# Token-table products ahead of the last early shared step, and their weighted one-hots written by ScalarE, in a two-layer attention and mixture-of-experts kernel

## The reference, cut to what matters

```python
logits = xf @ router_w.T + router_b
top_vals, top_idx = jax.lax.top_k(logits, K)          # K = 4 of E = 32
rw = jax.nn.softmax(top_vals, axis=-1) * SCALE
combine = jnp.einsum('tke,tk->te', jax.nn.one_hot(top_idx, E), rw)
g = silu(einsum('th,eih->tei', xf, gate_w)); u = einsum('th,eih->tei', xf, up_w)
routed = jnp.einsum('tei,ehi,te->th', g * u, down_w, combine)
shared = silu(xf @ shared_gate_w.T) * (xf @ shared_up_w.T) @ shared_down_w.T
return routed + shared
```

## Time and profile before

| | us |
|---|---|
| median of 3 runs | 398.67 (398.26, 398.67, 399.49) |
| the profiled execution | 398.21 |
| its span, from first to last instruction | 396.4 |
| busy: PE, DVE, ACT, POOL | 330.4, 271.0, 194.0, 180.7 |
| mean granted TensorE clock | 0.952 of full speed |

### The profile page before, as it was taken

How to read it: one execution, slowest core, us unless ns; L and a number is a source line. 1 busy time by engine, 2 the same in 40 slices (tenths; PEclk the granted TensorE clock), 3 DMA queues, 4 the chain that set the end, 5 groups by cost and what they waited for, 6 DMA issues and landing times.

```text
span 396.4 us, 8440 instructions
## 1 busy us (share of the span) xinstructions
PE 330.4 (83%) x2392; PEld 193.7 (49%) x2392; DVE 271.0 (68%) x842; ACT 194.0 (49%) x452; POOL 180.7 (46%) x321
## 2 busy tenths in 40 slices
PE   0007877777999999999999959999877689998997
PEld 0006763443455555555555756666553345554455
DVE  2998869724676766666667596999877246677374
ACT  1349544335455555555551047999921255552110
POOL 2000002266677777777744145666600547774200
PEclk9999957989999999999999979999995899999999
DMA  8999999616933333333563679910011213331441
GB/s 240 345 253 340 251 336 247 166 55 180 310 106 98 105 99 108 107 102 97 131 219 134 239 262 276 223 44 2 2 50 58 79 53 95 109 94 63 155 154 53
DMA packets 35038, 59.88 MB, mean 151 GB/s; under 512 B 4178, under 2 KB 23346, under 8 KB 34994
## 3 DMA queue, kind: packets, MB, share of 16 engines
q1 hardware_dynamic: 26850, 40.41, 34.9%
q0 software_dynamic: 6528, 17.83, 14.8%
q10 hardware_dynamic: 1616, 1.11, 1.0%
HBM read 47.28 MB, written 12.06 MB: 150 GB/s over the span
## 4 chain that ended last, share of the span: by engine, by line
PE 63%; DVE 15%; issue 6%; DMA 5%; POOL 5%; ACT 5%; DVEq 1%; ACTq 0%; SPq 0%; POOLq 0%
PE bank L1388 21%; PE bank L1417 7%; PE bank L1249 6%; PE bank L1431 4%; PE bank L1400 4%; PE bank L1370 4%; PE bank L1482 3%; PE bank L1470 3%; DMA xg<-m_xn,tab 2%; POOL xg L515 2%; PE bank L1262 2%; DMA x_sb<-x 2%; DVE x_sb L1068 1%; PE bank L1162 1%; PE bank L1288 1%
## 5 line engine op out<-in xcount | busy, mean ns | idle before, releaser
L1388 PE MATMUL bank<-arena,xT 128*64 x272 | 94.4, 491 | 2.2 <-ACT xT L647 2.2
L1390 PE MATMUL bank<-xn,xT 128*64 128x384 f32 (+1 forms) x272 | 94.5, 492 | 0.0
L515 POOL DMA_INDIRECT xg<-m_xn,tab x68 | 66.2, 973 | 52.4 <-DVE tab L909 24.8
L504 POOL DMA_INDIRECT m_ys<-ysb,dest x68 | 67.8, 997 | 34.7 <-issue 18.0
L636 ACT ACTIVATE xn<-arena 128x768 f32 (+1 forms) x68 | 56.2, 827 | 18.3 <-issue 17.8
L1388 PEld LDWEIGHTS bank<-arena,xT 128*64 128x64 f32 x272 | 35.0, 139 | 43.9 <-issue 43.9
L992 DVE COPY ysb<-bank 128x256 f32<-128x256 f32 x68 | 26.1, 420 | 39.3 <-PE bank L1433 39.1
L654 ACT ACTIVATE sg<-bank 128x192 f32<-128x192 f32 (+1 forms) x71 | 22.7, 319 | 37.6 <-PE bank L1390 31.7
L647 ACT ACTIVATE xT<-bank 128x512 f32<-128x512 f32 (+1 forms) x36 | 21.3, 592 | 36.0 <-PE bank L1370 36.0
L959 DVE COPY xn<-arena 64x256 f32 (+1 forms) x136 | 36.6, 307 | 1.0
L1417 PE MATMUL bank<-arena,hT 128*64 x136 | 35.0, 380 | 1.7 <-DVE dn L955 1.7
(11 more groups left out here) (197 smaller groups left out, 664.8 us busy)
## 6 DMA issues: line engine op xcount, KB each, us to landing
arena<-w_gu SPq DMA_DIRECT2D x3, 3456.0 KB, 21.9
arena<-m_ys SPq DMA_DIRECT2D x8, 512.0 KB, 5.8
arena<-w_dn SPq DMA_DIRECT2D x6, 576.0 KB, 14.1
arena<-w_gu SPq DMA_DIRECT2D x2, 1408.0 KB
arena<-w_dn SPq DMA_DIRECT2D x3, 864.0 KB, 22.4
m_xn<-xn SPq DMA_DIRECT2D x2, 1024.0 KB, 9.8
arena<-m_ys SPq DMA_DIRECT2D x8, 256.0 KB, 3.3
arena<-w_dn SPq DMA_DIRECT2D x7, 192.0 KB, 9.5
```

Source lines behind the costliest of these rows:

```text
L504: nc.gpsimd.indirect_dma_start(out=ys_d[L.name], out_offset=bass.IndirectOffsetOnAxis(ap=dest[:, s:s + 1], axis=0), in_=ysb[:, s % BUFS, : ...
L515: nc.gpsimd.indirect_dma_start(out=xg[:, b, :], out_offset=None, in_=xn_d[L.name], in_offset=bass.IndirectOffsetOnAxis(ap=d["tab"][:, s:s ...
L1388: T.matmul(out[0:BLOCK, 0:2 * J2], xT[:, s % 4, c, 0:BLOCK], arena[:, bass.ds(off + c * 2 * J2, 2 * J2)], start=(c == 0), stop=(c == C - 1 ...
L1390: ins = T.matmul(out[BLOCK:P, 0:2 * J2], xT[:, s % 4, c, BLOCK:P], gu2[:, s % 2, cols], start=(c == 0), stop=(c == C - 1), tile_position=( ...
```

## The change

PE runs iterations 1 to 3 of the early steps, then the 32 products of the token table, then iteration 4 (turn and down of step 3), then the 24 products as before. DVE no longer writes `tok1` for the first mixture. ACT does, with eight copies scaled by a column of `tokid`, one per token tile, 128 x 192 each: four behind the y copy of n = 1, four behind that of n = 2. ACT waits for `til1` (`til_ready`); PE waits for all eight copies (`tok_ready`) before the products. The second mixture keeps its order.

```diff
@@ early_shared on ScalarE
                     if n >= 1:
                         act.wait_ge(q["d_done"], n)
                         nc.scalar.activation(ysb[:, n - 1, :], bank[7][:, 0:H], ACT.Copy).then_inc(q["y_copied"], 1)
+                    if n in (1, 2):
+                        act.wait_ge(til_ready, 1)
+                        til, tok = (RS[L.name][w].rearrange("p (t k) m -> p t (k m)", t=NT) for w in ("til1", "tok1"))
+                        for t in range(NT // 2 * (n - 1), NT // 2 * n):
+                            nc.scalar.activation(tok[:, t], til[:, t], ACT.Copy, scale=tokid[:, t:t + 1]).then_inc(tok_ready, 1)
@@ routing on VectorE
-                link(V.tensor_tensor(r["til1"], iota16[:, 0:L.tiles].unsqueeze(1).broadcast_to([P, NT * K, L.tiles]),
-                                     d["tf"][:].rearrange("p t k -> p (t k)").unsqueeze(2).broadcast_to([P, NT * K, L.tiles]),
-                                     ALU.is_equal))
                 til, tok = (r[w].rearrange("p (t k) m -> p t (k m)", t=NT) for w in ("til1", "tok1"))
-                V.tensor_tensor(tok, til, tokid[:].unsqueeze(2).broadcast_to([P, NT, K * L.tiles]), ALU.mult)
+                ins = V.tensor_tensor(r["til1"], iota16[:, 0:L.tiles].unsqueeze(1).broadcast_to([P, NT * K, L.tiles]),
+                                      d["tf"][:].rearrange("p t k -> p (t k)").unsqueeze(2).broadcast_to([P, NT * K, L.tiles]),
+                                      ALU.is_equal)
+                if L is L0:
+                    ins.then_inc(til_ready, 1)
+                else:
+                    link(ins)
+                    V.tensor_tensor(tok, til, tokid[:].unsqueeze(2).broadcast_to([P, NT, K * L.tiles]), ALU.mult)
@@ routing on TensorE
                 if L is L0:
-                    shared_steps(L, "early", 0, N, 1, N + 1)
+                    shared_steps(L, "early", 0, N, 1, N)
                 else:
...
+                if L is L0:
+                    pe.wait_ge(tok_ready, NT)
                 for a in range(NT * K):
...
                 ins.then_inc(m["tokens"], 1)
+                if L is L0:
+                    shared_steps(L, "early", 0, N, N, N + 1)
```

More of the change, by code:

```diff
@@ L295, in mk_xattn_ffn @@
         kth_done, dest_ready = sem("kth_done"), sem("dest_ready")
+        til_ready, tok_ready = sem("til_ready"), sem("tok_ready")
         block = es.enter_context(nc.Block())
```

## The result

The changed kernel is a little faster, and by how much depends on the count. Over all 22 executions of each, the medians are 399.20 us against 399.78, a ratio of 0.9985, and the means 398.67 against 399.98. The ratio on record is 0.9932, 95% interval 0.9904 to 0.996. So 0.9932 overstates the gain. By each count the sign is the one forecast; the forecast of -1.0 us lies between -0.6 (medians) and -2.7 (0.68% of 398.67), and the means say -1.3.

A forecast was written before the change was run, and what follows sets the result against it. PE's own list (early steps, table, choices, after step) was taken as the bound. Order -0.4 and half the clock's fall -0.6 make -1.0, from a median of 398.67 to 397.7 us; range 396.6 to 398.9.

The forecast's parts named there:

- the forecast of -1.0 us: Whole kernel: order -0.4 and half the clock's fall -0.6, from a median of 398.67 to 397.7 us.
- PE's own list sets the start of the tile stage: Early steps to tile stage: the end depends on when PE finishes its list; first tile turn at 84.5 to 85.7.
- POOL's product 2 is held by a chunk and ends 0.63 late: Early steps: product 2 waits out DVE's chunk 2 and ends at 73.35, not 72.72.
- Order 0.4 and clock 1.2: PE's list up to the after step's silu: 1.6 us earlier, 0.4 by order, 1.2 by a clock staying at 2.4 GHz.
- The copies are covered: ACT in the early steps: two batches of four copies, 1.45 us each, delay no `hT_out`; 0.27 at the upper bound.
- The idle time is PE's wait for product 3: Ahead of the last early turn: PE idles 1.01 us for POOL's product 3; the table products fill it.
- Half of the clock's price for the median: Token table stretch: the clock's fall costs 1.2 us in the profile; 0.6 counted for the median.
- The rival that the gathers are the bound: Tile stage: the table comes 2.9 us earlier and all of it shows, 395.8 us; chance 0.05.
- That POOL gets no turn between chunks: Early steps rival: product 2 waits for all four chunks, 1.73 us late, giving 400.0 us; chance 0.08.

The follow-up runs named there:

- e6: Changed kernel with PE's order taken further: 24 products and the after step's gate and up ahead of the last early down; median 397.02 us, ratio 0.9933.
- e7: e6 with the weighted one-hots kept on VectorE, no copies on ScalarE; median 396.02 us, ratio 0.9923 to the kernel before.
- e5: The repeat: changed kernel run again, nothing altered, for a second profile; median 398.46 us, ratio 0.9938 to the kernel before.
- e2: The copies alone: changed kernel with PE's order of before; median 400.12 us, ratio 0.9987 to the kernel before.
- e1: The order alone: kernel before with PE's new order, weighted one-hots still on VectorE; median 398.24 us, ratio 0.9935.
- e8: Changed kernel with unread identity products in PE's waits, 14 in the first mixture's routing, 16 in the second's; median 397.01 us, ratio 0.9921.
- e10: e6, with ScalarE's copies, plus the unread products of e8; median 396.12 us, ratio 0.9892 to the kernel before.
- e4: Changed kernel with pos1 of the first mixture in eight chunks instead of four; median 399.65 us, ratio 0.9984 to the kernel before.
- e3: Kernel before with six unread identity products on PE in the wait ahead of the last early turn; median 400.91 us, ratio 0.9986.
- The three pairs above: Without copies against with: e1 and e5 (398.24, 398.46), e7 and e6 (396.02, 397.02), e7 plus e8's unread products and e10 (394.67, 396.12).
- the woven order: PE's order of e6, also used in e7; from table products to first tile turn 6.38 us in e6, for 8.10.

## Why the prediction was right

Step by step, in the profile that it was made for:

- *PE's own list sets the start of the tile stage.* Right. POOL had 1.55 us to spare ahead of gather 4, and e6 brought the first tile turn 1.72 nearer to the table products with the gathers left alone. In e6 and e7 POOL's addition ahead of gather 4 follows gather 3 without such a wait, so there the gathers and PE's list are about even.
- *POOL's product 2 is held by a chunk and ends 0.63 late.* Right: it ended at 73.46 (I had 73.35 in the clock of a profile in which `til1` began 0.14 sooner), 0.45 behind the end of chunk 2. The cause is shown by the ends of all 24 products that met such an instruction.
- *Order 0.4 and clock 1.2.* The sum is right: the first tile turn came 1.85 earlier, counted from `til1`, for 1.6. What was mis-sized are the products at 2.4 GHz: 32 took 0.82 to the next start (I had 0.97), 24 took 0.62 (0.72), together 0.25; so the first tile turn came at 84.34, a little ahead of the 84.5 to 85.7 that I had named. PE's two waits for products 2 and 3 fell by 0.40 (0.40 and 1.01 before, 1.01 and none after). The clock didn't fall behind the table products, in this profile or in that of e5. That the new order keeps it up is not shown: it didn't fall in e2 either, which has the old order, and it fell at 78.8 in e1, which has the new one. So of the 1.85 us 0.40 is shown to be the order's; the rest is a clock that didn't fall, and that the change is why stays open.
- *The copies are covered.* Right in the profile made for it and in size (1.50 and 1.48 for 1.45), but wrong as a rule. The cover is there in the course of that profile, with the clock back at 2.4 GHz at 68 us. With the clock back at 74.0 PE stood 0.21 for `hT_out` (e5). At 2.4 GHz in the first early steps PE comes sooner, the wait for `til1` that I had put at nothing is 1.84 us, and PE stands 1.68 (e8, e10); with the chunks shortened it stood 0.36 and 0.40 (e4). "What is queued behind the waiting instruction" was the right question, asked for one course of the clock only.
- *The idle time is PE's wait for product 3.* Right in that profile, but not of the kernel as such. In e2 and e5 product 3 took 0.59 and there was nothing to wait for, in e3 hardly anything, and e2 and e5 show the order worth nothing then. It depends on which DVE instruction a product meets, and that on how fast the early steps ran.
- *Half of the clock's price for the median.* The size can't be settled by these runs: -0.6 by medians, -2.7 by the ratio, -1.5 in the repeat (398.46 against 399.95). That the forecast of -1.0 lies among them is in part luck: against the one profile of the kernel before, the stage was 1.85 ahead in one execution and 0.23 in the other, by the clock in the early steps, and no step of the prediction asks how often each happens. What I had not counted is that the rest of the kernel, 308 to 314 us of the same code, moves by more than the change is worth. So 2.3 of the 4.0 us between the two profiled spans are no gain of this stage.

The rival that the gathers are the bound fell, by the 1.55 us at gather 4 and by the repeat, where the table products stood 1.39 earlier than before and the first tile turn only 0.23. That POOL gets no turn between chunks fell, by product 2. Still open is whether the earlier tile stage makes a good course of the clock later on more frequent: the best of the changed kernel's 34 executions, 394.19, is under the best of the kernel before beside them (396.63), but nothing here shows a mechanism.

On the two rules drawn on: the Trainium skill, page "TensorE: Matmul & The Clock Gate", section "Part 1: The HAM clock gate (the "warmup" mystery)", says that the point of the change differs between runs of one kernel. The profiles agree, with the clock back at 2.4 GHz at 68 us in one execution of the changed kernel and at 74 in another. The Trainium skill, page "ScalarE: Activation LUTs", section "Rules for kernel authors", would have the product on VectorE; its figure is for operations with a single source, and this product has two. The three pairs above lean that way, by 0.2 to 1.5 us of the median. What the traces show behind it is ACT's queue: copies of 1.5 us ahead of an `hT_out` that PE waits for.

## What to carry to other kernels

Work that no one waits for yet belongs into a wait that stands on the bound engine anyway; look for such waits on that engine's own list (here 0.47, 0.81 and 1.01 us) before moving work between engines. A piece of work moved to an idle engine is free only if nothing behind it in that engine's queue is wanted sooner when the other engines run faster: ask it for each course of the clock that a profile could show, the fastest above all, not for the one at hand. And where the clock can fall, compare a stage with the same stage, counted from an instruction that both kernels have, and not two spans; and do it between executions whose clock ran alike up to there, as e2 and e5 did, since the changed kernel's first tile turn was 1.85 us ahead in one execution and 0.23 in another, against one and the same profile of the kernel before.

## What was not expected of the hardware

One kernel's time moved by up to 10 us between executions, and the mean granted clock went with it: among the changed kernel's 22 it was 0.956 for the three at 394.2 to 394.3 and 0.935 for all above 400. Unread products in PE's waits raised it to 0.961 to 0.978 over all runs of e8, and with the woven order without copies gave the fastest kernel of this study, 394.67.

VectorE's one-hot instructions and GpSimd's products, all with two operands in SBUF, took turns, whole instruction by whole instruction: a product of 0.59 us alone took 0.73 to 1.66, ending 0.44 to 0.45 behind the end of the VectorE instruction that it met in 24 cases of 24, and a chunk that came next grew from 1.21 to 1.60 us.
